# The 32x32 matmuls of an attention step in four rounds over the array's squares, with the small turns of the next step ahead of them

## The chip, the cores and the metric

One Trainium2 chip, one of its cores. The metric is the device time of one execution of the whole kernel in microseconds (us).

## The reference

The input x is 8 images of 256 channels and 96 x 96 pixels, float32. One layer is computed from it:

```python
xh = x.transpose(0, 2, 3, 1)
win = xh.reshape(B, H // WS, WS, W // WS, WS, C).transpose(0, 1, 3, 2, 4, 5).reshape(-1, L, C)   # L = 144
qkv = (win @ qkv_w.T + qkv_b).reshape(-1, L, 3, HEADS, HD).transpose(2, 0, 3, 1, 4)              # 8 heads of 32
attn = jnp.einsum('bhld,bhmd->bhlm', q, k) * SCALE
attn = jax.nn.softmax(attn + bias[None], axis=-1)
out = jnp.einsum('bhlm,bhmd->bhld', attn, v).transpose(0, 2, 1, 3).reshape(-1, L, C)
out = out @ proj_w.T + proj_b
x_lpe = (conv2d(x, lpe_w, groups=C, pad=1) + lpe_b) * lpe_scale * noise_mask
freq2 = dct2(x_attn_img + x_lpe)
x_freq = idct2(freq2 * sigmoid(5.0 * (abs(freq2) - freq_mean)))
y = batchnorm(conv2d(x + x_freq, fr_w), bn2_g, bn2_b)
return gelu(y)
```

Ahead of it stands a mask from the energy of dct2(x). The change touches the two products of the attention alone: the scores q k^T of each head in each 12 x 12 window of 144 pixels, and the output P v.

## The kernel before, in words

The kernel runs a mask stage over all images first, then for each image an attention stage and a frequency stage, and at the end normalises and applies gelu. The engines run programs of their own and meet through semaphores.

**The attention stage.** A strip is 12 rows of the image. A *step* G is two windows side by side (v = 0, 1) and four of the eight heads (j = 0..3); there are 8 strips of 8 steps, T = 0..7 in each strip, 64 steps in an image, 512 in all. Heads have 32 channels, so a head's q and k lie on 32 partitions, 32j to 32j+31, and its products use a 32x32 *square* of TensorE's array: its row is given by the partitions that are read (r), its column by the partitions of PSUM that are written (c); I write (r, c). A window has 144 queries, 128 of them in four chunks of 32 and the last 16, the *few*.

TensorE's part of step G (`step`, L1374 to L1426), in its program's order:

- the q piece for a later step (`piece`), a matmul of 128x128 with 288 columns for each half of the channels;
- `transposes(G, 0)` and `(G, 1)`: the normalised probabilities turned, 128x128, with a projection of the strip before (`project`) between; `side_transposes(G)`;
- the k piece, the turn of finished rows (`turn`), the v piece;
- `attend(G)` (L1305): the output of all 128 later keys, 8 matmuls of 128x32 (all rows, one column of squares each) into `psO[v]`, left open for accumulation;
- `attend_few(G)` (L1317): the remaining 16 keys' share of the output, 8 matmuls of 32x32 and 144 columns, on squares (j, j), for v = 0 and then v = 1. The last raises `av`, on which ScalarE's `o_out` (L662, evicting at L666) waits;
- `wait_apart(pe, *free)` (L1422): one group of waits for what the scores overwrite or read: the eviction of the turned rows (`zt_out`, ScalarE L674), the sum of the projected rows (`z_done`) and the eviction of the k piece (`taken(("k", ...))`, ScalarE L640). Not all of them exist in every T. The helper works out values in registers first and then waits;
- `score(Y)` with Y = G + 3 (L1269): for each v 4 matmuls of the few queries, on squares (j, 3-j), into `psF`, and then for each v 16 matmuls, all (j, c), into `psS[j][v]`. The last raises `scores`, on which VectorE's `scores_out` (L913 on, L926) waits;
- `few_transposes(G + 1)` (L1296), called *the small turns* here: a wait of its own for GpSimd's `norm_done`, then 4 matmuls of 32x32 and 16 columns, on squares (3-j, j), which raise `few_ps`.

So the 48 matmuls of 32x32 and 144 columns in a step come as (j, j) for v = 0 and 1, the wait, (j, 3-j) for v = 0 and 1, all 16 squares for v = 0, all 16 for v = 1. Every matmul is float32 and stands in the trace as two loads of weights and two matmul records, called passes below; all of them are recorded under L1148, the helper `mmul`.

**The other engines.** VectorE: `recip(G+1)` (L934), `scores_out(G+2)` in 9 chunks (bias and minimum, L926), `pt_out(G)`, and steps of a depthwise convolution. ScalarE: `o_out(G-1)`, 9 exponentials (L650), the copies of transposed probabilities (L660), the evictions of the pieces and of the turned rows. GpSimd: `normalise(G+1)`, which waits for VectorE's reciprocal: L503, two L507 (what the small turns read), L510.

In the opening of an image `score(0)` to `score(2)` run with pieces between; the last three steps of an image have no score.

Of the kernel before, what the change touches and what calls it, by code (L numbers as in the profile page):

```python
# [25 lines left out]
C, H, W = 256, 96, 96  # L26
HEADS, WS, HD = 8, 12, 32
L = WS * WS
HL = L // 2
CT = C // 128  # L30
HG = 4
# [38 lines left out]
def build(nc, a, out, B):  # L70
# [7 lines left out]
    with ExitStack() as ctx:  # L78
# [161 lines left out]
        def few_row(j):  # L240

            return 32 * (HG - 1 - j)
# [903 lines left out]
        def _(pe):  # L1146
# [81 lines left out]
            def attention(b):  # L1228
# [40 lines left out]
                def score(X):  # L1269

                    hg = X % 2
                    for v in range(2):
                        for j in range(HG):
                            at = few_row(j)
                            mmul(psF[at:at + 32], q_sb[32 * j:32 * j + 32, hg, 2 * L + 32 * v:2 * L + 32 * v + 32],
                                 k_sb[32 * j:32 * j + 32, hg, L * v:L * v + L], start=v == 0, stop=v == 1)
                    for v in range(2):
                        for j in range(HG):
                            for c in range(HG - 1, -1, -1):
                                last = mmul(psS[j][v][32 * c:32 * c + 32],  # L1280
                                            q_sb[32 * j:32 * j + 32, hg, L * v + 32 * c:L * v + 32 * c + 32],
                                            k_sb[32 * j:32 * j + 32, hg, L * v:L * v + L])
                    last.then_inc(S["scores"], 1)
# [33 lines left out]
                def attend_few(G):  # L1317

                    P, hg = G // 2, G % 2
                    for v in range(2):  # L1320
                        at = 2 * C + CT * HD * v + HD * hg
                        for j in range(HG):
                            few = slice(32 * j, 32 * j + 32)
                            last = mmul(psO[v][few], v_sb[P % 2][few, at:at + HD], ptf[few, :],
                                        start=False, stop=True)
                    last.then_inc(S["av"], 1)
# [23 lines left out]
                def opening(between, freed):  # L1350
# [8 lines left out]
                    score(0)  # L1359
# [6 lines left out]
                    score(1)  # L1366
# [4 lines left out]
                    score(2)  # L1371
                    few_transposes(0)

                def step(G):  # L1374
# [40 lines left out]
                    attend_few(G)  # L1415
# [7 lines left out]
                    if Y is not None:  # L1423
                        score(Y)
                    if G + 1 < NG64:
                        few_transposes(G + 1)  # L1426

# [165 lines left out]
```

## Time and profile before

| | |
|---|---|
| median of 3 runs | 7872.96 us (7866.91 to 7875.8) |
| the profiled execution's own time | 7864.25 us |
| its span, first to last instruction | 7862.7 us |
| TensorE busy, share of the span | 7125.1 us, 91% |
| ScalarE, VectorE, GpSimd busy | 5120.4, 4789.3, 2482.0 us |
| mean granted TensorE clock | 0.965 |

A matmul record's duration runs from its start to a modelled end, several run at once, and so the time that a group of small matmuls costs is read from starts. "PEld" is the loading of weights. "issue" is a pause for which the profile shows no cause in another engine, which includes the sequencer's own waits.

### The profile page before, as it was taken

The page shows a single profiled execution, that of the slowest core. Times are in us where ns is not written, and L with a number is a line of the kernel's source. Part 1 is how long each engine was busy: PE and PEld are TensorE (multiplying, and loading weights), DVE is VectorE, ACT ScalarE, POOL GpSimd, SP SyncE. Part 2 cuts the span into 40 slices and gives each one's busy share as a digit, 9 for nine tenths or more (in the row PEclk, how much of TensorE's full clock was granted, in tenths as well). Part 3 has the DMA queues.
Part 4 walks back from the last instruction along what each step waited for, and adds up shares of the span by engine and source line. Part 5 has one row for each costly group of instructions (what it writes and reads, how often), then busy time and mean ns, then how long its engine had stood idle before and what let it go on. Part 6 is the DMA issues. An engine that isn't in the chain of part 4 may idle for free.

```text
span 7862.7 us, 278400 instructions
## 1 busy us (share of the span) xinstructions
PE 7125.1 (91%) x101938; PEld 5635.5 (72%) x101938; DVE 4789.3 (61%) x16580; ACT 5120.4 (65%) x16972; POOL 2482.0 (32%) x3894
## 2 busy tenths in 40 slices
PE   9999899999999999999999999999999999999910
PEld 8999577777777777777777777777777777777700
DVE  4555577457754776477746775577547764777400
ACT  5555688548764886477746775588648864886444
POOL 1111344324431443144323443244314431443200
PEclk9999999999999999999999999999999999999955
DMA  7554010020103100301021100201031003000299
GB/s 129 98 98 91 19 33 25 30 91 32 33 19 101 33 25 29 97 26 33 31 63 52 33 25 31 95 26 33 19 101 33 29 24 97 27 32 17 75 386 405
DMA packets 406440, 525.98 MB, mean 67 GB/s; under 512 B 252768, under 2 KB 355648, under 8 KB 388800
## 3 DMA queue, kind: packets, MB, share of 16 engines
q1 hardware_dynamic: 388864, 431.63, 18.8%
q0 software_dynamic: 16320, 77.56, 2.5%
q8 instruction: 793, 12.99, 0.7%
q14 instruction: 463, 3.79, 0.2%
HBM read 357.18 MB, written 151.95 MB: 65 GB/s over the span
## 4 chain that ended last, share of the span: by engine, by line
PE 82%; ACT 6%; DMA 4%; DVE 4%; issue 3%; SPq 0%; ACTq 0%; DVEq 0%; POOL 0%; POOLq 0%
PE ps L1148 74%; PE ps L1288 5%; ACT work L650 3%; DMA AH<-y_scratch 3%; DVE work L926 2%; PE ps L1346 2%; DMA out<-AH 2%; ACT work L660 1%; PE ps L1294 1%; PE ps L1293 1%; DVE xs L979 0%; ACT work L640 0%; DVE work L1053 0%; ACT AH L674 0%; DVE work L979 0%
## 5 line engine op out<-in xcount | busy, mean ns | idle before, releaser
L650 ACT ACTIVATE work<-work 128x144 f32<-128x144 f32 x4608 | 1854.6, 410 | 779.4 <-DVE work L926 779.4
L1148 PE MATMUL ps<-work 32*32 32x144 f32 (+2 forms) x57478 | 1453.9, 289 | 57.9 <-issue 23.5
L979 DVE SCALAR_TENSOR_TENSOR work<-xs,lw,work 128x570 f32<-128x570 f32 (+1 forms) x1920 | 1446.7, 807 | 0.0
L926 DVE CUSTOM_DVE_ANT_0 work<-ps,negbias 128x144 f32<-128x144 f32 x4608 | 1092.7, 305 | 498.6 <-PE ps L1148 496.7
L1148 PEld LDWEIGHTS ps<-work 32*32 32x32 f32 (+1 forms) x57478 | 1085.9, 104 | 377.1 <-issue 341.6
L503 POOL TENSOR_TENSOR work<-work 128x128 f32<-128x128 f32 x512 | 209.1, 408 | 3312.7 <-DVE work L934 3312.7
L1148 PE MATMUL ps<-work,wqkv 128*128 128x288 f32 x4096 | 1227.1, 422 | 28.1 <-issue 26.6
L510 POOL TENSOR_TENSOR work<-work 128x1152 f32<-128x1152 f32 x512 | 1086.9, 2123 | 0.0
L650 ACT ACTIVATION_READ_ACCUMULATOR work<-work 128x1 f32 x4608 | 893.1, 194 | 0.0
L1148 PEld LDWEIGHTS ps<-work,wqkv 128*128 128x128 f32 x4096 | 705.9, 192 | 169.2 <-issue 39.0
L1148 PE MATMUL ps<-dct,AH 96*96 96x97 f32 (+1 forms) x7168 | 781.2, 261 | 9.7 <-ACT AH L570 9.2
L1148 PEld LDWEIGHTS ps<-inv,work 96*96 96x96 f32 (+1 forms) x5632 | 630.4, 173 | 207.5 <-issue 161.0
L1288 PEld LDWEIGHTS ps<-eye,work 128*128 128x128 f32 x4096 | 498.5, 141 | 362.7 <-ACT work L660 170.5
L1148 PEld LDWEIGHTS ps<-dct,AH 96*96 96x96 f32 (+1 forms) x7168 | 737.5, 178 | 20.1 <-ACT AH L570 11.8
L1288 PE MATMUL ps<-eye,work 128*128 128x128 f32 x4096 | 630.7, 277 | 131.0 <-ACT work L660 123.8
L543 POOL TENSOR_TENSOR work<-work 96x384 f32<-96x384 f32 x512 | 421.1, 822 | 920.7 <-DVE work L1047 920.7
L660 ACT ACTIVATE work<-ps 128x512 f32<-128x512 f32 x1024 | 613.7, 599 | 115.6 <-PE ps L1288 113.0
L1148 PE MATMUL ps<-wqkv,work 128*32 128x64 f32 (+1 forms) x6144 | 633.5, 279 | 0.0
L1148 PE MATMUL ps<-inv,work 96*96 96x96 f32 (+1 forms) x5632 | 627.8, 256 | 0.0
L1148 PE MATMUL ps<-AH,work 128*128 128x384 f32 (+2 forms) x2188 | 608.3, 514 | 9.2 <-DVE work L883 4.7
L1047 DVE TENSOR_SCALAR work<-ps 96x384 uint32<-96x384 uint32 x512 | 283.7, 554 | 521.2 <-PE ps L1148 521.2
L779 ACT ACTIVATE AH<-ps 128x768 f32<-128x768 f32 x192 | 155.6, 810 | 662.0 <-PE ps L1148 662.0
(145 smaller groups left out, 10903.3 us busy)
## 6 DMA issues: line engine op xcount, KB each, us to landing
work<-in_x SPq DMA_DIRECT2D x128, 576.0 KB, 5.3
xs<-in_x SPq DMA_DIRECT2D x64, 1152.0 KB, 5.7
AH<-in_x SPq DMA_DIRECT2D x192, 384.0 KB, 3.4
y_scratch<-AH SPq DMA_DIRECT2D x192, 384.0 KB, 2.5
AH<-y_scratch SPq DMA_DIRECT2D x64, 1152.0 KB, 23.5
out<-AH POOLq DMA_DIRECT2D x64, 1152.0 KB, 17.4
work<-mask_scratch SPq DMA_DIRECT2D x128, 288.0 KB, 3.5
xs<-in_x SPq DMA_DIRECT2D x112, 96.0 KB, 5.5
```

The lines of the kernel that those rows point to most:

```text
L503: g.tensor_tensor(early[i], sp[i][:, 0:2 * HG, 0:FEW], rden[i][:, 0:2 * HG].unsqueeze(2).broadcast_to([128, 2 * HG, FEW]), ALU.mult).then_ ...
L510: g.tensor_tensor(sp[i][:, :, FEW:L], sp[i][:, :, FEW:L], rden[i].unsqueeze(2).broadcast_to([128, LC, 128]), ALU.mult).then_inc(S["norm_do ...
L543: g.tensor_tensor(tg[q % 2][0:96], tg[q % 2][0:96], msb[q // 4 % 2][0:96, 4 * (q % 4):4 * (q % 4) + 4].unsqueeze(2) .broadcast_to([96, 4, ...
L650: o = act.activation(sp[i][:, c, :], sp[i][:, c, :], ACT.Exp, scale=-1.0, bias=mn[i][:, c:c + 1], accum_out=den[i][:, c:c + 1])
L660: act.activation(pt[:, v, :, 0:128], psTM, ACT.Copy).then_inc(S["pt_a"], 1)
L779: act.activation(ys[par], ps[:, 4 + 2 * par:6 + 2 * par, 0:384], ACT.Copy).then_inc(S["y_ready"], 1)
L926: v.tensor_tensor_reduce(out=sp[i][:, c, :], in0=psF if j == HG else psS[j][w], in1=negbias[:, X % 2, j, :], scale=1.0, scalar=BIG, op0=AL ...
L979: v.scalar_tensor_tensor(dst[:, ct, :, w0:w1], xs[side][:, ct, y0 + dy:y0 + dy + HS, w0 + dx - 1:w1 + dx - 1], lw[:, ct, tap:tap + 1], dst ...
L1047: v.tensor_scalar(tg[par][0:96].rearrange("p c l -> p (c l)").bitcast(U32), ps[0:96, 2 + par, 0:384].bitcast(U32), 0x7FFFFFFF, None, ALU.b ...
L1148: return nc.tensor.matmul(o, l, r, start=start, stop=stop)
L1288: last = nc.tensor.transpose(psTM[:, j, :], sp[G % 3][:, 2 * j + v, FEW:L], eye[:])
L1346: last = nc.tensor.transpose(ps[0:96, bank, 128 * i:128 * i + 128], branch(strip_at, half)[:, ct, r - HS * half, :], eye[:])
```

## The change

The two groups of 32x32 matmuls are merged and put in another order. `score` is split into `few_score(X, v)` and `main_score(X, v, shared)`, where `shared` takes the 8 squares with c = j or c = 3 - j, or the 8 others; `attend_few` is split by v; and `squares(G, X)` issues:

1. v = 0: (j, j) of the output, (j, 3-j) of the few queries' scores, the 8 other squares of the scores: 16 squares, each once;
2. v = 1: the same;
3. v = 0: the 8 shared squares of the scores;
4. v = 1: the same, raising `scores`.

`attend_few` now stands behind the group of waits instead of ahead of it, and `few_transposes(G + 1)`, its wait included, stands ahead of the 48 instead of behind them. The order of the chunks within a head also changes, from c = 3..0 to rising.

```diff
--- before.py
+++ after.py
@@ -1266,21 +1266,36 @@
 
                     pe.wait_ge(*read(X, n))
 
-                def score(X):
+                def few_score(X, v):
 
                     hg = X % 2
-                    for v in range(2):
-                        for j in range(HG):
-                            at = few_row(j)
-                            mmul(psF[at:at + 32], q_sb[32 * j:32 * j + 32, hg, 2 * L + 32 * v:2 * L + 32 * v + 32],
-                                 k_sb[32 * j:32 * j + 32, hg, L * v:L * v + L], start=v == 0, stop=v == 1)
-                    for v in range(2):
-                        for j in range(HG):
-                            for c in range(HG - 1, -1, -1):
+                    for j in range(HG):
+                        at = few_row(j)
+                        mmul(psF[at:at + 32], q_sb[32 * j:32 * j + 32, hg, 2 * L + 32 * v:2 * L + 32 * v + 32],
+                             k_sb[32 * j:32 * j + 32, hg, L * v:L * v + L], start=v == 0, stop=v == 1)
+
+                def main_score(X, v, shared):
+
+                    hg = X % 2
+                    for j in range(HG):
+                        for c in range(HG):
+                            if (c in (j, HG - 1 - j)) == shared:
                                 last = mmul(psS[j][v][32 * c:32 * c + 32],
                                             q_sb[32 * j:32 * j + 32, hg, L * v + 32 * c:L * v + 32 * c + 32],
                                             k_sb[32 * j:32 * j + 32, hg, L * v:L * v + L])
-                    last.then_inc(S["scores"], 1)
+                    return last
+
+                def squares(G, X):
+
+                    for v in range(2):
+                        if G is not None:
+                            attend_few(G, v)
+                        if X is not None:
+                            few_score(X, v)
+                            main_score(X, v, False)
+                    if X is not None:
+                        main_score(X, 0, True)
+                        main_score(X, 1, True).then_inc(S["scores"], 1)
 
                 def transposes(G, v):
 
@@ -1314,16 +1329,16 @@
                             mmul(psO[v][32 * j:32 * j + 32], v_sb[P % 2][:, ch:ch + 32], pt[:, v, j, :],
                                  start=True, stop=False)
 
-                def attend_few(G):
+                def attend_few(G, v):
 
                     P, hg = G // 2, G % 2
-                    for v in range(2):
-                        at = 2 * C + CT * HD * v + HD * hg
-                        for j in range(HG):
-                            few = slice(32 * j, 32 * j + 32)
-                            last = mmul(psO[v][few], v_sb[P % 2][few, at:at + HD], ptf[few, :],
-                                        start=False, stop=True)
-                    last.then_inc(S["av"], 1)
+                    at = 2 * C + CT * HD * v + HD * hg
+                    for j in range(HG):
+                        few = slice(32 * j, 32 * j + 32)
+                        last = mmul(psO[v][few], v_sb[P % 2][few, at:at + HD], ptf[few, :],
+                                    start=False, stop=True)
+                    if v == 1:
+                        last.then_inc(S["av"], 1)
 
                 def project(m, u, bank, strip_at):
 
@@ -1356,19 +1371,19 @@
                     between[2]()
                     piece(("q", 1, 0), 5)
                     wait_apart(pe, (S["q_pad"], b + 1), taken(("k", 0, 0)))
-                    score(0)
+                    squares(None, 0)
                     freed()
                     piece(("k", 1, 0), 6)
                     piece(("v", 0, 0), 7)
                     made_out(("q", 1, 0))
                     piece(("q", 0, 1), 5)
                     wait_apart(pe, taken(("k", 1, 0)), read(0, LC))
-                    score(1)
+                    squares(None, 1)
                     piece(("k", 0, 1), 6)
                     made_out(("v", 0, 0))
                     piece(("v", 1, 0), 7)
                     wait_apart(pe, taken(("k", 0, 1)), read(1, LC))
-                    score(2)
+                    squares(None, 2)
                     few_transposes(0)
 
                 def step(G):
@@ -1412,7 +1427,6 @@
                         made_out(made[0])
                         piece(i, bank_of(i))
                     attend(G)
-                    attend_few(G)
                     free = [(S["zt_out"], m * NU + turned + 2)] if turned is not None else []
                     if Y is not None and projected is not None:
                         free.append((S["z_done"], m * NU + projected + 1))
@@ -1420,10 +1434,9 @@
                         free.append(taken(("k", Y % 2, Y // 2)))
                     if free:
                         wait_apart(pe, *free)
-                    if Y is not None:
-                        score(Y)
                     if G + 1 < NG64:
                         few_transposes(G + 1)
+                    squares(G, Y)
 
                 def rows():
 
```

## Rows read from the trace of the kernel before

**Rows 1.** The page: busy times; the chain that ended last, by engine and line.
```profile
PE 7125.1 (91%) x101938; PEld 5635.5 (72%) x101938; DVE 4789.3 (61%) x16580; ACT 5120.4 (65%) x16972; POOL 2482.0 (32%) x3894
...
PE 82%; ACT 6%; DMA 4%; DVE 4%; issue 3%; SPq 0%; ACTq 0%; DVEq 0%; POOL 0%; POOLq 0%
```

**Rows 2.** Groups of instructions by shape on TensorE: busy us, mean ns | idle before.
```profile
L1148 PE MATMUL ps<-work 32*32 32x144 f32 x49152 | 1129.3, 289 | 48.8 <-issue 23.5 <-ACT AH L674 15.6 <-ACT work L640 5.3
...
L1148 PE MATMUL ps<-fold,work 32*32 32x16 f32 x4096 | 157.8, 181 | 9.6 <-issue 9.6
```

**Rows 3.** Timeline of weight loads, step A: start us, length us, what, xcount, [idle before].
```profile
2609.32 1.72 PEld L1148 LDWEIGHTS ps<-work 32*32 32x32 f32 x96 [0.22 <-issue]
2611.01 0.27 PEld L1148 LDWEIGHTS ps<-fold,work 32*32 32x32 f32 x8
2611.31 0.30 PEld L1148 LDWEIGHTS ps<-work,wqkv 128*128 128x128 f32 x2
```

**Rows 4.** The same timeline, step B.
```profile
2617.77 0.40 PEld L1148 LDWEIGHTS ps<-work 32*32 32x32 f32 x16 [0.23 <-issue]
2618.38 1.34 PEld L1148 LDWEIGHTS ps<-work 32*32 32x32 f32 x80 [0.21 <-issue]
2619.68 0.27 PEld L1148 LDWEIGHTS ps<-fold,work 32*32 32x32 f32 x8
2619.98 0.30 PEld L1148 LDWEIGHTS ps<-work,wqkv 128*128 128x128 f32 x2
```

**Rows 5.** The same timeline, step C.
```profile
2654.08 1.34 PEld L1148 LDWEIGHTS ps<-work 32*32 32x32 f32 x80 [0.59 <-issue]
...
2655.69 0.30 PEld L1148 LDWEIGHTS ps<-work,wqkv 128*128 128x128 f32 x2
```

**Rows 6.** Timeline of ScalarE around the waits of steps A, B and C.
```profile
2609.04 0.59 ACT L674 ACTIVATE AH<-ps 96x512 f32<-96x512 f32 x1
...
2610.18 0.54 ACT L666 ACTIVATE work<-ps,qb 128x288 f32<-128x288 f32 x1
2611.96 0.42 ACT L650 ACTIVATE work<-work 128x144 f32<-128x144 f32 x1 [1.25 <-DVE work L926]
...
2617.72 0.59 ACT L674 ACTIVATE AH<-ps 96x512 f32<-96x512 f32 x1
...
2653.42 0.59 ACT L674 ACTIVATE AH<-ps 96x512 f32<-96x512 f32 x1
```

**Rows 7.** Timeline of VectorE, end of step A.
```profile
2610.47 0.20 DVE L934 RECIPROCAL work<-work 128x9 f32<-128x9 f32 x1
2611.61 0.31 DVE L926 CUSTOM_DVE_ANT_0 work<-ps,negbias 128x144 f32<-128x144 f32 x1 [0.94 <-PE ps L1148]
```

**Rows 8.** Weight loads under way in stretches from 2610.40 (step A): stretch, us, busy (xcount), clock, DMA.
```profile
2610.40:2610.53 0.13, 0.12 (x7) 1.00 0.25 92
2610.40:2610.65 0.25, 0.23 (x8) 1.00 0.25 94
2610.40:2610.91 0.51, 0.48 (x37) 1.00 0.28 96
2610.40:2611.06 0.66, 0.63 (x40) 1.00 0.25 88
```

**Rows 9.** Timeline of GpSimd, end of step A.
```profile
2610.74 0.41 POOL L503 TENSOR_TENSOR work<-work 128x128 f32<-128x128 f32 x1 [3.70 <-DVE work L934]
2611.14 0.68 POOL L507 TENSOR_SCALAR work<-work,side 128x16 f32<-128x16 f32 x2
```

**Rows 10.** As rows 8, from 2609.72, the first scores of step A.
```profile
2609.72:2609.90 0.18, 0.18 (x11) 1.00 0.23 87
2609.72:2610.05 0.33, 0.33 (x25) 1.00 0.22 85
```

**Rows 11.** Timeline of weight loads, step D.
```profile
1690.05 1.53 PEld L1148 LDWEIGHTS ps<-work 32*32 32x32 f32 x96 [0.23 <-issue]
```

## The prediction

> **What bounds the kernel now.** Four views, in this order. The page first: TensorE is busy 91% of the span and its work is 82% of the chain that ended last, 74% under one line, the helper that records every matmul [rows 1]. The groups by shape say which matmuls those are: the 32x32 ones of 144 columns are 49152 records, two passes for each of 24576 matmuls. That is 512 steps (64 for each of 8 images) with 48 each: 8 of the few queries' share of the output, 8 of their scores, 32 of the other scores; the 16-column ones are the small turns, 4 matmuls in a step [rows 2]. The time of one record (289 ns) is a latency; records overlap. So the cost has to be read from starts, and the timeline of the weight loads gives them, one load per pass.
>
> I read three steps of one image, A, B and C, and one more, D. In A, 96 loads (16 passes for the few queries' output, 80 for the scores) run without a break from 2609.32, the turns' loads come at 2611.01 and the next piece at 2611.31 [rows 3]. In B the 16 loads of the output come at 2617.77, then 0.21 us pass in which nothing starts, then the 80 of the scores from 2618.38 take 1.34, and the next piece is at 2619.98 [rows 4]. In C that pause is 0.59 us, and the 80 take 1.34 again [rows 5]. The pause is the wait ahead of `score(Y)`. ScalarE's rows name what it ends on: the eviction of the turned rows (L674) ends at 2618.31 in B and 2654.01 in C, both 0.07 ahead of the first score load; in A it ends at 2609.63, so the scores could load from 2609.70, just when the 16 output passes are through [rows 6]. ScalarE did this work because TensorE's own piece and turn had ended, so the moment is fixed against TensorE, not against the last step. Hence TensorE's stream with that one hole is the bound, and what a step saves behind the hole is saved from the time, step for step. VectorE is not: it sits idle 0.94 us before it takes the new scores at 2611.61 [rows 7]. The clock is at its upper level, granted 1.00 in these stretches [rows 8].
>
> **What the change removes and moves.** Three edits.
>
> 1. The 16 passes of `attend_few` leave the shadow of the wait and go behind it. Today they cost nothing in B and C (they end inside the hole) and about 0.4 us in A, where the wait ends with them. After it, TensorE idles from the end of `attend` to the end of the wait, and all 96 score and output passes stand behind it.
>
> 2. The turns (4 matmuls, 8 passes of 16 columns) and their wait move ahead of the 48. Today the wait costs nothing: TensorE's sequencer reaches it while passes are queued. Now it comes second after the first wait with nothing queued. No row shows such a wait alone; the nearest is the 0.07 us from ScalarE's end to a load [rows 6]. Below nothing it cannot be; above, twice 0.1 with its register arithmetic. I take 0.10. What it waits for is long there: VectorE's reciprocal at 2610.47 starts GpSimd, whose two L507 operations end at 2611.82, and the turns that read them are those of step B, at 2618.5 [rows 7, 9]. The turns themselves: 4 matmuls at the pace of point 3, 0.07 us. At the end they lay in the drain of the scores (last 32x32 passes to the next 128x128 load): that drain stays, so I credit nothing for their going there.
>
> 3. The 48 in rounds. What a load costs when squares do not collide is shown in A at the last round of 16 matmuls, all on different squares: the count of loads goes from 8 to 37 between 2610.65 and 2610.91, 29 loads in 0.26 us, 9 ns each. Its last pass starts by 2611.05, 0.40 after its first; less the 0.145 by which a second pass follows its first, 15 matmuls took 0.255, 17 ns each [rows 8]. Just before stands the other thing: 1 load in 0.12 us [rows 8], a load that waits for a square still busy. A square is busy for two passes of 0.12 us (144 columns twice, as the four-square groups of the output show: 16 passes in 0.40, [rows 4]) and some 0.02 for a load that could not be hidden (the 0.145 is one pass and that), 0.27 together.
>
> Check the rule on the old order: 39 starts at 17 ns are 0.66, the last second pass adds 0.145, and a square that comes again after 4 matmuls (0.07) waits 0.17 to 0.20, twice (second set of few scores, first main score): 1.15 to 1.21. Measured is 1.34. So the rule leaves out 0.13 or more, about the stalled stretch of rows 8, which comes from shared squares met in the middle of a set.
>
> The new order: 47 starts at 17 ns are 0.80, plus 0.145. Round two repeats a square after 16 matmuls, 0.27, just when it is free: no wait. Round three meets the diagonal after 16 and the other shared squares after 13 or so: 0.03. Round four meets all eight after 8 matmuls, 0.14, and waits 0.13 once. Sum R = 1.11 us from the first load of the rounds to the last start. Its bounds: below, a shared square holds four matmuls, 4 x 0.245 less the last pass, 0.86; above, the pace at which the old order goes when nothing holds it: in step D the wait was over early and all 96 loads took 1.53 [rows 11].
>
> The Trainium skill ("TensorE: Matmul & The Clock Gate", Part 3, the span model) would have tiles on different squares start some 4 ns apart. By it the 96 passes are never short of issue, and R would be near 0.9 (an estimate). The rows give 9 ns a load on different squares, twice that, so the sum keeps 17 ns a matmul.
>
> **The sum.** From the last start to the next piece's load 0.25 us pass (load of the last pass ends 2619.72, last start about there, next piece 2619.98). So the new next piece loads at: end of wait + 0.07, + 0.10 second wait, + 0.07 turns, + R + 0.25.
> A: 2609.63 + 0.07 + 0.10 + 0.07 + 1.11 + 0.25 = 2611.23, against 2611.31: 0.08 less.
> B: 2618.31 + 0.07 + 0.17 + 1.36 = 2619.91, against 2619.98: 0.07 less.
> C: 2654.01 + 0.07 + 0.17 + 1.36 = 2655.61, against 2655.69: 0.08 less.
> All three break even at R = 1.18 to 1.19. Steps with scores are 61 in each image, 488 in all: 488 x 0.077 = 37 us. The 24 scores of the openings and the 24 steps without scores change by a tenth of a microsecond each, with either sign: nothing. The profiled execution took 7864.25 (span 7862.7); less 37 that is 7827. The median of the runs, 7872.96, lies 8.7 above it: 7836.
>
> **Costed at nothing, with their cover.** `av` rises later: today ScalarE's L666 runs in A from 2610.18, and ScalarE then waits 1.25 us until 2611.96 for VectorE's first chunk [rows 6]. After it, the second diagonal set starts 0.27 into the rounds (2609.87 + 0.27), ends some 0.5 later (two passes and a latency of 0.28), so L666 ends near 2611.2, still 0.7 ahead. If that cover goes, the transposes of the next step wait for L666. `few_ps` rises earlier than `scores` instead of after it, which lets VectorE start up to 0.05 us earlier; VectorE is not late, so nothing. Queued behind the moved norm wait on TensorE is everything (all rounds), but its value is 6 us old.
>
> **The rivals.**
> *The stalls stay* (ends slower). The 0.13 that the rule misses in the old order comes back once in the new one, at the eight shared squares of round three or four; R = 1.25 (rounded), 0.065 worse than break even: 488 x 0.065 = 32 us more, 7905. For it: the old order shows stretches in which one busy square holds back loads for free ones, and the 0.4 us of cover are gone in any case. Against: no square is met in the middle of a round. It decides from R = 1.19. Its far end is D's pace: R = 1.53, 488 x 0.34 = 166 us, 8039: the order would not matter, issue would.
> *Issue never binds.* Then the busy squares alone bind, R is the lower bound of 0.86 and 0.04 to reach the last shared square, 0.90: gain 0.28 a step, 137 us, 7736. Against it: after the first hold of the old order, with loads queued, 14 loads take 0.15 us from 2609.90 to 2610.05, no faster than 9 ns each [rows 10]. The span model above, in the Trainium skill's page, would have it so.
> *Even*: R between 1.15 and 1.21, within 16 us of 7873. The terms of 0.10 for the wait and 0.07 for the turns decide it as well as R.
> That the change does not do what it says (squares collide within a round) I exclude: the sets (j, j), (j, 3-j) and the other eight are disjoint by the row and column of each tile.
>
> **How the numbers follow.** 0.2% is 16 us here, about what a measurement of this kernel can tell from no change. My forecast (gain of 37, with R from 1.02 to 1.15) has 0.42, issue never binding 0.08, even 0.16, stalls stay 0.28, D's pace 0.06. Faster: 0.42 + 0.08 = 0.50; within: 0.16; slower: 0.34. The range leaves out D's pace and issue never binding, and reaches part of the way to each: 7765 to 7940. It is as wide as it is since cases of both signs hold it; the forecast's own range is 7790 to 7856.
>
> **What would show it.** In the changed kernel: no 32x32 load between the end of `attend` and the eviction's end; turns' loads within 0.2 us of that end (point 2); 96 loads in a row that take 1.1 to 1.2 us (point 3), with the first 64 at 9 ns and one stall near the end; next piece 0.07 us earlier in each of A, B and C; L666 after the rounds' first half, and no wait of a transpose for it. I am wrong if the 96 take over 1.2, or if the turns start over 0.2 us after the wait's end.

## The result: slower by 0.9%

The changed kernel takes **7940.45 us**, median of 4 runs (7934.46 to 7947.51), beside 7871.49 (7866.91 to 7875.8) for the kernel before: ratio **1.0088 [1.0071, 1.0106]**, some 69 us more. Forecast were 7836 us and 0.50 for faster; the time lies just above the range (7940) and on the side of the rival *the stalls stay*. The profiled execution took 7934.46 (span 7932.8, mean granted clock 0.965 as before), 70 more than that of before.

The page of the changed kernel, the lines that answer to [rows 1], and ScalarE's exponential:

```profile
PE 6925.7 (87%) x101938; PEld 5382.5 (68%) x101938; DVE 4773.8 (60%) x16580; ACT 5168.5 (65%) x16972; POOL 2485.3 (31%) x3894
...
PE 64%; ACT 17%; issue 12%; DMA 4%; DVE 2%; ACTq 1%; POOL 0%; SPq 0%; DVEq 0%; POOLq 0%
...
L650 ACT ACTIVATE work<-work 128x144 f32<-128x144 f32 x4608 | 1854.2, 410 | 450.4 <-DVE work L926 450.4
```

TensorE's share of the chain falls from 82% to 64%, ScalarE's rises from 6% to 17% and "issue" from 3% to 12%. That is the wait ahead of the 48 matmuls laid bare: TensorE now stands idle until ScalarE's eviction ends, so the chain passes through ScalarE, most of all through its exponentials (L650, 10% of the span, before 3%). Over a whole step ScalarE still has time to spare: it sits idle 450 us ahead of the exponentials (779 before) and 332 us ahead of L666 (21 before). In the stretch ahead of the eviction it has none: up to B's eviction it works without a pause from its copy of the first transposed probabilities on, from 2628.41 to 2633.70. That is 5.29 us, as it was before the change (2613.02 to 2618.31), and at its end TensorE waits for it. The waits of TensorE's matmuls, most costly first (releaser: us in total, times, longest):

```profile
PE ps L1148 <- ACT AH L674: 166.5, 317, 1.0
PE ps L1148 <- issue: 159.8, 178, 5.1
```

Before, the same releaser had 21.1 us ahead of L1148 in all, 15.6 of them ahead of the 32x32 matmuls [rows 2].

The timeline of weight loads (start, length, what, xcount, [idle before]) in the steps that answer to A, B and C of [rows 3 to 5]:

```profile
2625.01 0.15 PEld L1148 LDWEIGHTS ps<-fold,work 32*32 32x32 f32 x5 [0.61 <-issue]
2625.06 0.10 PEld L1148 LDWEIGHTS ps<-work 32*32 32x32 f32 x1
...
2625.09 1.38 PEld L1148 LDWEIGHTS ps<-work 32*32 32x32 f32 x93
2626.69 0.30 PEld L1148 LDWEIGHTS ps<-work,wqkv 128*128 128x128 f32 x2 [0.23 <-issue]
...
2633.76 0.15 PEld L1148 LDWEIGHTS ps<-fold,work 32*32 32x32 f32 x5 [0.84 <-issue]
2633.82 0.10 PEld L1148 LDWEIGHTS ps<-work 32*32 32x32 f32 x1
...
2635.45 0.30 PEld L1148 LDWEIGHTS ps<-work,wqkv 128*128 128x128 f32 x2 [0.23 <-issue]
...
2673.92 0.15 PEld L1148 LDWEIGHTS ps<-fold,work 32*32 32x32 f32 x5 [1.21 <-issue]
2673.98 0.10 PEld L1148 LDWEIGHTS ps<-work 32*32 32x32 f32 x1
...
2675.61 0.78 PEld L1148 LDWEIGHTS ps<-work,wqkv 128*128 128x128 f32 x4 [0.23 <-issue]
```

ScalarE, around A and B, and its eviction in C:

```profile
2624.34 0.59 ACT L674 ACTIVATE AH<-ps 96x512 f32<-96x512 f32 x1
...
2626.02 0.53 ACT L666 ACTIVATE work<-ps,qb 128x288 f32<-128x288 f32 x1 [0.42 <-PE ps L1148]
2627.25 0.42 ACT L650 ACTIVATE work<-work 128x144 f32<-128x144 f32 x1 [0.70 <-DVE work L926]
...
2628.41 0.60 ACT L660 ACTIVATE work<-ps 128x512 f32<-128x512 f32 x1 [0.26 <-PE ps L1303]
...
2633.11 0.59 ACT L674 ACTIVATE AH<-ps 96x512 f32<-96x512 f32 x1
...
2673.27 0.59 ACT L674 ACTIVATE AH<-ps 96x512 f32<-96x512 f32 x1
```

Read A: the eviction ends at 2624.34 + 0.59 = 2624.93, the turns load at 2625.01, the rounds from 2625.06, the next piece at 2626.69. From the eviction's end to the next piece that is 1.76 us; in B (2633.70 to 2635.45) and C (2673.86 to 2675.61) 1.75. Before it was 1.68, 1.67 and 1.68 [rows 3 to 6]. So each step loses 0.07 to 0.08 instead of gaining as much.

The weight loads under way in stretches that all begin ahead of the turns of A (stretch, us, busy (xcount), clock, DMA), to be held beside [rows 8]:

```profile
2624.97:2625.17 0.20, 0.17 (x32) 1.00 0.22 60
2624.97:2625.40 0.43, 0.40 (x42) 1.00 0.12 31
2624.97:2625.51 0.54, 0.49 (x42) 1.00 0.09 25
2624.97:2625.79 0.82, 0.76 (x72) 1.00 0.06 16
2624.97:2625.86 0.89, 0.83 (x76) 1.00 0.06 15
2624.97:2625.97 1.00, 0.93 (x76) 1.00 0.05 13
```

32 loads are through in 0.2 us: 16 matmuls that had been queued during the wait, 4 turns and 12 of the rounds. Only 10 follow in the next 0.23 us, and none from 2625.40 to 2625.51; then 30 come in 0.28 us, 9 ns each, which is the pace of point 3; then 4 more, and again none from 2625.86 to 2625.97. In starts over all steps: 16 matmuls at 17 ns, then one whose two passes lie 0.12 us apart with nothing else loading, some 0.46 us for each 17 with the pause until the next burst (in step A from 1115 to 1575 ns behind the last start of `attend`). **The pace of 17 ns a matmul is there, but only for about 16 matmuls at a time, and between them the stream stops.** The slow stretch begins after 12 of the 48, and none of the first 16 shares a square with another of them; the turns' four squares come again in matmuls 5 to 8, which are among the 12. So a busy square is no reason for this first slow stretch.

**Where the 70 us are.** I cut each of the 488 steps with scores at the last start of `attend` and at the next piece (starts of all records, summed). The section between them takes 1221.3 us before and 1278.5 after, 57 more; the rest of the steps 2978.1 and 2996.4, 18 more; the openings and the frequency stages give back 5. Two things make up these 75. The ordinary step is some 0.075 us longer, the mean over T of the differences of the medians (the section at T = 2 and 6 2.210 and 2.293, at T = 3 and 5 2.450 and 2.516, at T = 1 2.455 and 2.582; the differences go from 0.034 at T = 0 to 0.127 at T = 1): 488 x 0.075 = 37 us. And there are **long pauses**, over 0.7 us between two starts of TensorE with no wait: 46 with 69.9 us before, 65 with 107.2 us after, 37 more. (Six of them, 4 to 5 us each, stand at the change of image in both kernels.) The one of step 12 in the second image, in both kernels (timeline of loads, after; then before):

```profile
1799.81 0.96 PEld L1148 LDWEIGHTS ps<-work 32*32 32x32 f32 x57
1803.10 0.21 PEld L1148 LDWEIGHTS ps<-work 32*32 32x32 f32 x12 [2.33 <-issue]
```

```profile
1790.20 1.52 PEld L1148 LDWEIGHTS ps<-work 32*32 32x32 f32 x84
1792.64 0.14 PEld L1148 LDWEIGHTS ps<-work 32*32 32x32 f32 x4 [0.92 <-issue]
```

2.33 us in the middle of the 48, where it was 0.92 near their end. The DMA share of the changed kernel from 1799.5 to 1803.1, in 40 slices, with the queues that moved something:

```profile
DMA  0000000000000600000000000000000000000000
...
q8 instruction: 1, 0.02, 1.6%
```

One packet of instruction code, in the slice that begins at 1800.67, and TensorE's last start ahead of the pause is at 1800.77. Taken narrowly, as pauses of over 0.7 us between two 32x32 passes behind a step's wait, there are 33 with 37.0 us before and 44 with 62.7 us after. Each of these has one such packet that began ahead of it, 0.5 to 1.6 us before and 0.02 to 1.7 us after the change; a few others of 0.8 us, four of them within a projection before the change, have none in the 6 us ahead of them. A packet alone does not make a pause: in 31% of the sections of before one began within a given stretch of 1.7 us (the one that ends 1 us behind the last start of `attend`), and 33 of the 488 have a pause. The number of packets in the whole run is the same in both (793).

### The profile page after: what moved, and what is told of

It reads as the page before. It is cut to its first block, busy times and chain, and to the rows that moved or that the text cites. A ratio compares the mean times of both kernels' runs of the same rounds, so it can differ in the third digit from the quotient of the medians.

```text
span 7932.8 us, 278400 instructions
## 1 busy us (share of the span) xinstructions
PE 6925.7 (87%) x101938; PEld 5382.5 (68%) x101938; DVE 4773.8 (60%) x16580; ACT 5168.5 (65%) x16972; POOL 2485.3 (31%) x3894
## 4 chain that ended last, share of the span: by engine, by line
PE 64%; ACT 17%; issue 12%; DMA 4%; DVE 2%; ACTq 1%; POOL 0%; SPq 0%; DVEq 0%; POOLq 0%
PE ps L1148 58%; ACT work L650 10%; PE ps L1303 4%; DMA AH<-y_scratch 3%; ACT AH L674 2%; ACT work L660 2%; DMA out<-AH 2%; ACT work L640 2%; ACT work L637 0%; DVE work L992 0%; ACTq L649 0%; PE ps L1361 0%; DVE work L1053 0%; DVE work L979 0%; DVE xs L979 0%
## 5 line engine op out<-in xcount | busy, mean ns | idle before, releaser
L650 ACT ACTIVATE work<-work 128x144 f32<-128x144 f32 x4608 | 1854.2, 410 | 450.4 <-DVE work L926 450.4
L1148 PE MATMUL ps<-work 32*32 32x144 f32 (+2 forms) x57478 | 1258.1, 290 | 63.9 <-issue 50.3
L1148 PE MATMUL ps<-work,wqkv 128*128 128x288 f32 x4096 | 1234.1, 423 | 36.1 <-issue 35.3
L1148 PEld LDWEIGHTS ps<-work 32*32 32x32 f32 (+1 forms) x57478 | 924.9, 104 | 192.3 <-issue 156.9
L650 ACT ACTIVATION_READ_ACCUMULATOR work<-work 128x1 f32 x4608 | 892.9, 194 | 0.0
L1148 PEld LDWEIGHTS ps<-work,wqkv 128*128 128x128 f32 x4096 | 705.4, 192 | 269.1 <-issue 151.4
L1148 PE MATMUL ps<-dct,AH 96*96 96x97 f32 (+1 forms) x7168 | 781.1, 261 | 9.7 <-ACT AH L570 9.2
L1148 PEld LDWEIGHTS ps<-inv,work 96*96 96x96 f32 (+1 forms) x5632 | 629.5, 173 | 208.1 <-issue 161.4
L1303 PEld LDWEIGHTS ps<-eye,work 128*128 128x128 f32 x4096 | 502.4, 142 | 380.5 <-ACT work L660 170.5
L1303 PE MATMUL ps<-eye,work 128*128 128x128 f32 x4096 | 634.6, 278 | 135.6 <-ACT work L660 123.7
L1148 PEld LDWEIGHTS ps<-dct,AH 96*96 96x96 f32 (+1 forms) x7168 | 737.4, 177 | 20.1 <-ACT AH L570 11.8
L1148 PE MATMUL ps<-wqkv,work 128*32 128x64 f32 (+1 forms) x6144 | 633.4, 279 | 0.0
L1148 PE MATMUL ps<-inv,work 96*96 96x96 f32 (+1 forms) x5632 | 627.2, 255 | 0.0
L1148 PE MATMUL ps<-AH,work 128*128 128x384 f32 (+2 forms) x2188 | 606.9, 513 | 9.2 <-DVE work L883 4.7
```

The source lines that it names most:

```text
L650: o = act.activation(sp[i][:, c, :], sp[i][:, c, :], ACT.Exp, scale=-1.0, bias=mn[i][:, c:c + 1], accum_out=den[i][:, c:c + 1])
L1148: return nc.tensor.matmul(o, l, r, start=start, stop=stop)
L1303: last = nc.tensor.transpose(psTM[:, j, :], sp[G % 3][:, 2 * j + v, FEW:L], eye[:])
```

## The experiments

Starts are medians over the 488 steps; "the section" is the one just cut. The numbers of pauses are those over 0.7 us without a wait, in the wide sense; another drawing of the line moves them by a few. Two kernels have a single run and no interval, and are read from their traces.

**Old order, everything behind the wait.** The change without its rounds:

```diff
                     attend(G)
-                    attend_few(G)
 ...
-                    if Y is not None:
-                        score(Y)
                     if G + 1 < NG64:
                         few_transposes(G + 1)
+                    attend_few(G)
+                    if Y is not None:
+                        score(Y)
```

> Both moves (the output's 16 passes behind the wait, the small turns ahead) with the old order of the 48. In the changed kernel the 96 passes take 1.417 us from first to last start in every step. Theory 1 (a matmul that reaches a square still busy holds the stream behind it until its own second pass has started, some 0.15 to 0.18 us each time, otherwise 17 ns a matmul): order matters, 1.50 to 1.60 here, as 1.53 in step D of the kernel before; time above the changed kernel by 0.1 us x 488 = 50 us, near 7990. Theory 2 (the stream takes a fixed 29.5 ns a matmul in any order): 1.42 again and 7940. Both: the turns start when the scores started before.

7989.14 us, ratio 1.0149 [1.013, 1.0168]. From the first to the last of the 96 starts 1.485 us; 68 pauses, 114.7 us. The rounds are worth 0.068 us a step when all 48 stand behind the wait (1.485 to 1.417), and the moves cost more than that. The 1.485 lies below theory 1's 1.50 to 1.60 and above theory 2's 1.42, so the order counts, but less than theory 1 has it. The time meets theory 1's 7990, some 8 of its 49 us over the changed kernel being pauses.

**Only the turns ahead.** The kernel before with `few_transposes(G + 1)` ahead of `score(Y)`:

> The kernel before with the small turns and their wait ahead of the scores, nothing else. From the changed kernel's steps: the second wait costs nothing, turns 0.03 us in front, and the drain to the next piece falls from 0.26 to 0.21. So 0.02 us a step less, 8 to 10 us in all: 7862, ratio 0.999. If the second wait is what cost the changed kernel its time (rival), 0.1 us a step more, 7920.

7890.03, ratio 1.0018 [1.0008, 1.0028], some 14 us more. The 80 passes take 1.358 (before 1.320), the last start is 0.211 ahead of the next piece (before 0.261), the section 2.479 (2.447); 46 pauses as before. A gain of some 10 us was expected, and this move alone costs a little. The likely reason, which no run tests, is that the 4 turns take places among the 16 matmuls that are queued during the wait, so the scores' stream has 4 fewer of them. The rival, 7920 by the second wait, falls.

**Rounds of 40.** The change with `attend_few` put back ahead of the wait:

```diff
                     attend(G)
+                    for v in range(2):
+                        attend_few(G, v)
 ...
-                    squares(G, Y)
+                    squares(None, Y)
```

> The changed kernel with the output's passes back ahead of the wait, so the rounds hold 40 matmuls: 12, 12, 8, 8. Theory 2: 40 x 29.5 ns = 1.18 us for the 80 passes against 1.32 before, 0.16 a step less than before with the turns' 0.02, 78 us: 7795. Theory 1: a square of the first antidiagonal comes again after 12 matmuls (0.20 us, busy 0.27): held at round two, at round three, at round four: 39 x 17 ns + 0.145 + 3 x 0.16 = 1.29 us, 0.05 a step less than before, 24 us: 7847. Rival (moved cover cost nothing, rounds are what is slow): above 7872.

7832.45, ratio **0.9941 [0.9923, 0.9958]**. The 80 passes take 1.178, 29.5 ns a matmul, just as the 48 of the changed kernel (1.417 / 48) and as theory 2 has it. Its time of 7795 is missed: the median section is 0.145 shorter than before (2.302), the mean one only 0.090, 44 us in all, since the steps gain unequally and the pauses are longer. Its loads in A, where the order after the 16 output passes is turns, then rounds:

```profile
2597.46 0.40 PEld L1148 LDWEIGHTS ps<-work 32*32 32x32 f32 x16 [0.23 <-issue]
2597.87 0.18 PEld L1148 LDWEIGHTS ps<-fold,work 32*32 32x32 f32 x8
2597.95 1.17 PEld L1148 LDWEIGHTS ps<-work 32*32 32x32 f32 x80
2599.35 0.78 PEld L1148 LDWEIGHTS ps<-work,wqkv 128*128 128x128 f32 x4 [0.23 <-issue]
```

So the sign of the whole change hangs on the move of the output: the same rounds win when 16 passes keep their cover.

**Rounds of 40, turns last.** Against the kernel before, only the order of the 40 scores differs:

```diff
-                    if G + 1 < NG64:
-                        few_transposes(G + 1)
                     squares(None, Y)
+                    if G + 1 < NG64:
+                        few_transposes(G + 1)
```

> rounds_40 (7832, ratio 0.994) with the small turns back behind the scores: the score order alone is changed against the kernel before. Putting the turns last was worth 13 us in the pair of row0_apart and 14 us in turns_first against before. Expected 7818 and a ratio of 0.992 to 0.993, 80 passes in 1.16 to 1.18 us. If the turns ahead were neutral once the scores go in rounds: 7832.

7798.42, ratio **0.9905 [0.9889, 0.9922]**, below the 7818 expected. The 80 passes 1.143, the section 2.238 (before 2.447); 51 pauses, 83.9 us. In A:

```profile
2590.85 1.56 PEld L1148 LDWEIGHTS ps<-work 32*32 32x32 f32 x96 [0.23 <-issue]
2592.36 0.28 PEld L1148 LDWEIGHTS ps<-fold,work 32*32 32x32 f32 x8
2592.66 0.79 PEld L1148 LDWEIGHTS ps<-work,wqkv 128*128 128x128 f32 x4
```

The 96 loads of 1.72 [rows 3] are 1.56, and the next piece comes 1.81 after the first load, before 1.99.

**Other orders of the old kind.** Is it the order that sets the pace, and which? Three orders of the 40, each with the turns ahead as in the second experiment, so that 7890 is what they stand against. With few(v) for the 4 matmuls of the few queries, main(v, anti) for those of the 16 on squares (j, 3-j) or for the 12 others, the first spreads the squares that come twice:

```diff
+                    few(0)
+                    main(0, False)
+                    main(0, True)
+                    main(1, False)
+                    main(1, True)
+                    last = few(1)
```

> turns_first with the 40 score matmuls in another order: few v=0 (4), the 12 other squares v=0, antidiagonal v=0, the 12 others v=1, antidiagonal v=1, few v=1. A square comes again after 16 matmuls, and at the very end after 4. Theory 1: two marginal holds and one at the end: 0.80 less 8 x 17 ns = 0.66, + 0.145, + 0.20 at the end, + 0 to 0.3 for the marginal ones: 1.0 to 1.3 us; time 7720 to 7860. Theory 2: 1.18 us, 7795, the same as rounds_40.

7910.7, ratio 1.0042 [1.0027, 1.0057]; the 80 passes 1.358, the same to the nanosecond. Spreading them that way brings nothing; 50 pauses and 87.2 us make it longer. Both expectations fail: 1.358 is above theory 1's 1.0 to 1.3, and theory 2, the same 1.18 in any order, cannot hold.

The next keeps row 0 of the array from meeting a busy square until the end (a list of rows j as last argument), the third does the same for row 1:

```diff
+                    rest = [1, 2, 3]
+                    few(0, [0] + rest)
+                    main(0, False, [0] + rest)
+                    few(1, rest + [0])
+                    main(1, False, rest + [0])
+                    main(0, True, rest)
+                    main(1, True, rest)
+                    main(0, True, [0])
+                    last = main(1, True, [0])
```

> Small turns first and the output's passes ahead of the wait, as in rounds_40, but the 40 score matmuls ordered so that a matmul on squares of row 0 never meets its square busy except at the very end: few v=0 (row 0 first), 12 others v=0, few v=1 (row 0 last), 12 others v=1 (row 0 last), antidiagonal rows 1 to 3 for v=0 and v=1, then row 0's two. Theory 3 (formed from the starts of the five kernels so far: what holds the stream until its second pass is a matmul on row 0, here always (0,0) or (0,3), that meets a busy square; rows 1 to 3 wait without holding others): no hold before the end, 38 x 17 ns + two uses of (0,3) in a row: 1.00 to 1.08 us for the 80 passes against 1.18 in rounds_40; 0.13 x 488 = 63 us under rounds_40: 7770. Theory 1 (any busy square holds): the antidiagonal of rows 1 to 3 for v=1 comes 3 matmuls after v=0 and holds: 1.25 to 1.35, 7870 or above. Theory 2 (29.5 ns a matmul): 1.18, 7832.

> The same order with rows 0 and 1 exchanged, the control: row 1 is now kept apart, and row 0's antidiagonal matmul for v=1 comes 3 matmuls after its v=0. Theory 3: held there, some 0.2 to 0.3 us more than row0_apart: 1.2 to 1.35, 100 to 150 us over it. Theory 1: the same as row0_apart, both 1.25 to 1.35. Theory 2: 1.18 in both.

7917.0, ratio 1.0064 [1.0047, 1.008], and 7919.75, ratio 1.0067 [1.005, 1.0084]; the 80 passes 1.406 and 1.401. That is longer than in any other order of the 40, and the two rows are alike: that it is row 0 whose busy squares hold back the stream (theory 3) falls. Theory 1 had the sign and 1.25 to 1.35, too little; theory 2 fails again.

The order of row 0 with the turns left last, as in the kernel before:

> row0_apart with the small turns back behind the scores, as in the kernel before. turns_first was 0.03 us a step slower than the kernel before (14 us). If that comes from the turns alone (0.07 us in front, their squares being the first scores' own, against 0.05 less at the end), 10 to 15 us under row0_apart. If the turns' place only mattered by the squares of the first scores: the same.

7903.94, ratio 1.0044 [1.0027, 1.006]; the 80 passes 1.371 against 1.320 in the kernel before. It is 13 us under its twin, as expected, and worse than the kernel before without the turns ahead too.

**Rows the other way round.** The changed kernel with `for j in reversed(range(HG))` in `few_score`, `main_score` and `attend_few`: other squares meet, at the same places in the stream.

> The changed kernel (48 in four rounds, behind the wait) with rows 3, 2, 1, 0 in place of 0, 1, 2, 3 within every group. Every distance between two uses of a square in one round and the next stays at 16 for the first two rounds; row 0 comes last in each group, in round three 19 matmuls after its last use (no longer 13), in round four at the very end. Theory 3: the hold of round three goes, that of round two moves back: 1.417 falls to 1.2 to 1.3, 7860 to 7890. Theories 1 and 2: 1.42 within 0.05, 7940.

One run: 7933.83 (span 7932.3); 66 pauses, 102.5 us. R is 1.417 again, and of the 105 starts of step A (104 passes and the next piece) 94 lie within 2 ns of where they did. Some of them, in ns from the last start of `attend`, around two of the stops (953 to 1115, 1451 to 1575):

```
changed kernel   906 922 953 992 1016 1051 1068 1115 1123 1140 ... 1434 1451 1452 1468 1484 1511 1529 1575 1583 1600
rows reversed    906 922 954 992 1016 1050 1067 1115 1123 1140 ... 1441 1451 1452 1468 1485 1510 1563 1575 1583 1600
```

The stops go by the **place in the stream**, not by the row. That does not clear busy squares in the later rounds: in round three the first shared squares come again after 13 matmuls in one order and 12 in the other, and in round four after 8 in both.

**64 columns.** Rounds of 40 with the score matmuls of a step cut to 64 columns; this leaves the scores of the other 80 keys out. In effect, for a step's scores alone:

```diff
-                        k_sb[32 * j:32 * j + 32, hg, L * v:L * v + L]
+                        k_sb[32 * j:32 * j + 32, hg, L * v:L * v + 64]
```

> rounds_40 with every score matmul of a step 64 columns wide; the scores of the other 80 keys are left out. A square is then busy for 2 x 0.053 us and not 2 x 0.12. Theory 2 (the stream of instructions bounds the rounds, 29.5 ns a matmul, in runs of 16 at 17 ns and a stop): the 80 passes still take 1.0 to 1.18 us. Rival (busy squares bound the rounds): 4 uses of an antidiagonal square at 0.13 are 0.5 us, so 0.7 or less with 40 x 17 ns of issue.

One run: 7685.28. The 80 passes take 0.845 us, 21 ns a matmul, between what the two readings expected. Between stops the starts still follow at 17 ns a matmul; the stops are shorter. In its step A:

```profile
2554.76 0.40 PEld L1148 LDWEIGHTS ps<-work 32*32 32x32 f32 x16 [0.23 <-issue]
2555.17 0.18 PEld L1148 LDWEIGHTS ps<-fold,work 32*32 32x32 f32 x8
2555.25 0.94 PEld L1148 LDWEIGHTS ps<-work 32*32 32x32 f32 x80
2556.28 0.78 PEld L1148 LDWEIGHTS ps<-work,wqkv 128*128 128x128 f32 x4
```

So the stop grows with the columns, as if passes already issued had to end in it, and the 17 ns do not. The number of instructions is thus not the whole of it. With 64 columns a square is also free sooner, so this run does not part passes that must end from squares that must come free.

**Fewer, wider matmuls.** If the number of instructions in the stream is what costs, four chunks of a head need not be four matmuls: all 128 queries of a head can be one, on all four squares of its row. The old order otherwise, turns between the two shapes (abridged):

```diff
+                    few_transposes(G + 1)
                     for v in range(2):
                         for j in range(HG):
-                            for c in range(HG - 1, -1, -1):
-                                last = mmul(psS[j][v][32 * c:32 * c + 32],
-                                            q_sb[..., L * v + 32 * c:L * v + 32 * c + 32],
-                                            k_sb[..., L * v:L * v + L])
+                            last = mmul(psS[j][v], q_sb[..., L * v:L * v + 128],
+                                        k_sb[..., L * v:L * v + L])
```

> The order before, but the 32 matmuls of 32x32 squares are 8 of 32x128: one for each head and window writes all four chunks of 32 queries, so a row of squares works for one matmul and there are 64 loads and matmuls instead of 160 in a step's scores; the small turns stand between the few queries' scores and these. If the number of instructions is the bound (theory 2): few scores 0.39, a change of tile shape 0.1 to 0.2, 8 matmuls at 2 x 0.245 = 0.5 us: 1.0 to 1.1 us in all, against 1.32 + 0.15 before: 0.3 us a step, 150 us: 7720. Rival: loads of 128 columns (0.19 us against 0.10 in the trace) cannot be hidden, or the four rows don't run side by side: 8 x 0.25 = 2 us, 8200.

**7730.68** (7728.97 to 7731.99), ratio **0.9816 [0.98, 0.9832]**: faster than both kernels, 146 us less than before, with the whole reference computed. Its step A and its page:

```profile
2568.79 0.82 PEld L1148 LDWEIGHTS ps<-work 32*32 32x32 f32 x32 [0.23 <-issue]
2569.58 0.28 PEld L1148 LDWEIGHTS ps<-fold,work 32*32 32x32 f32 x8
2569.88 0.56 PEld L1148 LDWEIGHTS ps<-work 32*128 32x128 f32 x16
2570.58 0.78 PEld L1148 LDWEIGHTS ps<-work,wqkv 128*128 128x128 f32 x4
```

```profile
PE 7022.8 (91%) x77362; PEld 5479.2 (71%) x77362; DVE 4803.7 (62%) x16580; ACT 5125.0 (66%) x16972; POOL 2488.7 (32%) x3894
```

8 matmuls take the place of 32, 24576 fewer records, and take 0.49 us from first to last start. The mean section is 2.204 us (before 2.503): 488 x 0.299 = 146, as much as the medians of the runs differ by; the two profiled executions lie 133 apart, so the rest of the kernel gives some 13 back. Pauses fall from 46 to 13 (29.9 us), so some 40 of the 146 are theirs. On the way the change of shape costs: 0.26 us from the last few scores through the turns to the first wide matmul.

## Why the prediction was wrong, point by point

**What bounds the kernel: right, by another road.** TensorE's stream with the hole of the wait is the bound, and what a step loses behind the hole is lost from the time: with rounds of 40, turns last, the mean section falls by 0.163 us, which is 80 us over 488 steps, and the run by 78 (67 between the profiled executions). The reason given was that ScalarE evicts when TensorE's own piece and turn have ended. The turn ended long before the eviction of B began at 2617.72 [rows 6]:

```profile
2613.02 0.60 ACT L660 ACTIVATE work<-ps 128x512 f32<-128x512 f32 x1 [0.16 <-PE ps L1288]
...
2615.75 0.60 PE L1346 MATMUL ps<-eye,work 128*96 128x128 f32 x4
```

Between the turn's end at 2616.35 and the eviction lie 1.37 us of exponentials and the eviction of the k piece. What fixes the moment are the step's transposes, with ScalarE's unbroken work behind them: the eviction ends 3.86 to 3.87 us after the start of the last transpose at T = 2 to 6, and 4.24 or 4.25 at T = 7, in the kernel before, the changed one, both with rounds of 40 and the one with wide scores. So the moment is indeed fixed against TensorE, and the conclusion stands. The hole itself is ScalarE's order of work; whether an eviction placed ahead of the last exponentials would close it, no run tried.

**Point 1, the cover of the 16 output passes: right in kind.** No 32x32 load stands between `attend` and the eviction's end, and TensorE idles there for 0.61, 0.84 and 1.21 us. What its loss costs depends on the pace: at the forecast 17 ns a matmul 8 of them are 0.14, at the 29.5 measured they are 0.24 (1.417 against the 1.178 of rounds of 40). Between these two kernels lie 108 us by the medians; 488 x 0.213, the difference of the median sections, is 104.

**Point 2.** The second wait was sized at 0.10 and costs nothing: the turns load 0.08, 0.06 and 0.06 after the eviction's end, where the scores loaded at 0.07 [rows 6]. The turns take 0.05 to the first load of the rounds, not 0.07. Their place at the end was credited with nothing and had held some 0.05: the last start is now 0.21 ahead of the next piece, before 0.26 (I took 0.25). These three errors lie in the change's favour, 0.16 us a step.

**Point 3, the pace: this is the step that failed.** "47 starts at 17 ns" and with it R = 1.11. R is **1.417** in the median step. The 17 ns were read from one set of 16 matmuls with [rows 8], and they are true for a set: the rows above show the same 9 ns a load. What one set does not show is the stop after it, 0.46 us for 17 matmuls in all. My own bound above, step D's 96 loads in 1.53 [rows 11], was the sustained pace and stood in the text; the forecast took the pace of a window and the bound from the stream, where it should have been the other way. [Rows 8] even held the stop, "1 load in 0.12 us", and I gave it to a busy square by the rule for collisions. The 0.13 that the rule then missed in the old order I put down to more collisions. In rounds, with the turns last, the same 40 take 1.143, so what the old order adds to that pace is 0.18 of its 1.320.

With the measured terms the sum is 0.07 + 0.05 + 1.42 + 0.21 = 1.75 from the eviction's end to the next piece, and 1.75 is what B and C show. The break-even R, with the errors of point 2 mended, is 1.68 - 0.07 - 0.05 - 0.21 = 1.35 instead of 1.18.

The Trainium skill ("TensorE: Matmul & The Clock Gate", Part 1, the engine queue depths) gives TensorE's queue a depth of 64. The burst of 16 matmuls behind the wait, each of two loads and two passes, is 64 records, and agrees with that; that the later stops come by the same count is a likeness, and no run here shows that it is the reason. Its span model (Part 3) would have different squares some 4 ns apart; the rows give 17 ns a matmul (8 to 9 a load) in a stretch and 29.5 sustained, so the measurement decides against it for these float32 matmuls of two passes.

**The order does count, but on top.** With the same place of everything else the old order takes 0.18 more for 40 matmuls (1.358 and 1.178 with the turns ahead, 1.320 and 1.143 with them last) and 0.068 more for 48. So the idea of the change is right, and rounds alone are a gain of 0.95%. That the 0.18 is busy squares was not parted from other effects of order; the three other orders of 40, meant to spare squares, did no better than the old one.

**Not in the sum: the pauses.** Half of the loss, 37 of some 75 us, comes from longer and more pauses, 26 of the 37 between two 32x32 passes. I had treated the 46 of before as given. They are 65 to 68 in the three kernels where 52 matmuls with 208 records stand behind the wait in one stretch (the changed one, the old order moved, the rows reversed), 43 to 52 where 16 of the passes stand ahead of it, and 13 with 24 fewer matmuls a step. That they have to do with the arrival of code is read from the packets beside them; no run changed that alone, and it stays open.

**The rival.** *The stalls stay* had the sign, and its cause is not the one: it wanted eight shared squares to cost 0.13 once. Its far end came nearer (a pace that binds without shared squares), but was too hard on the order, and the run with 64 columns shows that the pace is not of instructions alone. *Costed at nothing*: L666 ended at 2626.55 in A, 1.62 after the eviction of L674, where 2611.2, 1.57 after, was expected; ScalarE still had 0.70 us idle behind it. That held but for little: over the whole run the transposes of L1303 waited 10.4 us for L666, where those of L1288 had waited 5.5.

**The sum of the three parts**, by medians of whole runs: rounds of 40 alone -78, turns ahead of them +34, the output moved behind the wait +108, together +64; measured +69, and the runs of before beside these kernels lie 5 us apart (7871.5 and 7876.6).

## What to carry to other kernels

Take the pace of a stream of small matmuls from the whole stream, not from a window of 16 in it: here 17 ns in a set and 29.5 over 40 or 48. Count the instructions ahead of their order: one matmul of 32x128 for four of 32x32 brought nearly twice what the best order did (146 us and 78). And before work is moved out from under a wait to mend something else, try the mending with the work left where it is covered; here that was the difference between -0.6% and +0.9%.

## What the runs showed that I had not expected

- A stream of 32x32 matmuls with 144 columns, in rounds over different squares, runs at 29.5 ns each, for 40 and for 48 of them; with 64 columns at 21. The stops lie at the same nanoseconds with the rows reversed. Why there is one after each 16 or 17 matmuls stays open.
- A second wait right behind a first one, with nothing queued, costs nothing that can be seen (0.06 to 0.08 us from the eviction's end to the first load with it, 0.07 without).
- Pauses of 0.8 to 2.6 us in the middle of a stream, with no engine that releases them and one packet of instruction code that began shortly before. They come in the same steps of the images (12, 30, 34, 42, 44 and 52, in the changed kernel also 37), and their number changes with the make-up of the stream.
- Four matmuls of 32x128 on the four rows run side by side: their passes start 7 ns apart, the second four 0.23 us after the first, then four every 0.12 us.
